# Single tiles of two edge stages fetched row by row from SP and ScalarE instead of GpSimd, with two smaller edits, in a four-layer graph network on one core

## What is computed

```python
# layer 2: one of 16 matrices by edge type, summed by destination
h_src = feat[src]
for r in range(num_rels):
    mask = etypes == r
    msg = msg + h_src * mask[:, None].astype(feat.dtype) @ weight[r]
out = jax.ops.segment_sum(msg, dst, num_segments=feat.shape[0])
# layer 3: a three-matrix network on every edge, then mean and maximum by node,
# then a three-matrix network on every node (W4, W5, W6)
m = jnp.concatenate([x[row], x[col], edge_attr], axis=1)
```

## Time and profile before

| | |
|---|---|
| median of three runs | 13071.3 us |
| the three runs | 13070.82, 13071.3, 13152.06 us |
| the profiled execution, its time | 13160.62 us |
| its span, from first to last instruction or transfer | 13158.9 us |
| PE busy | 2819.3 us (21%) |
| DVE busy | 6175.8 us (47%) |
| ACT busy | 1273.1 us (10%) |
| POOL busy | 9662.0 us (73%) |
| DMA, mean over the span | 84 GB/s |
| granted TensorE clock, mean | 0.558 of full speed |

### The profile page before, as it was taken

The page is one execution under the profiler, slowest core; times in us unless marked ns, Lnnn a source line. Parts: engine busy times, 40 slices in busy tenths (PEclk is TensorE's granted clock), DMA queues, the critical chain, the costliest instruction groups (busy, mean ns, idle before and its releaser), DMA issues. The chain is left out here.

```text
span 13158.9 us, 78994 instructions
## 1 busy us (share of the span) xinstructions
PE 2819.3 (21%) x12129; PEld 1989.0 (15%) x12156; DVE 6175.8 (47%) x21573; ACT 1273.1 (10%) x3641; POOL 9662.0 (73%) x10101
## 2 busy tenths in 40 slices
PE   2000011111100740000000000013444444444446
PEld 2000011111100420000000000012232332332233
DVE  8877357777733432222222222224555555555554
ACT  3111011111110320000000000000000000001011
POOL 7777757777777747777777777777777777777774
PEclk6555555555555665555555555555666666666665
DMA  5444334444443332222222222222222222222221
GB/s 168 119 118 115 108 106 118 117 116 118 115 119 108 124 103 66 65 66 64 67 64 67 64 67 64 67 51 55 66 66 66 66 64 66 65 66 66 66 66 32
DMA packets 731549, 1103.24 MB, mean 84 GB/s; under 512 B 240731, under 2 KB 347192, under 8 KB 730567
## 3 DMA queue, kind: packets, MB, share of 16 engines
q0 software_dynamic: 332944, 306.83, 12.6%
q1 hardware_dynamic: 231478, 567.25, 11.4%
q10 hardware_dynamic: 167040, 228.30, 5.7%
HBM read 548.64 MB, written 552.93 MB: 84 GB/s over the span
## 5 line engine op out<-in xcount | busy, mean ns | idle before, releaser
L130 POOL DMA_INDIRECT msg<-Y,idx x3125 | 2965.9, 949 | 1060.1 <-issue 951.8
L130 POOL DMA_INDIRECT g<-in_edge_attr,idxs x3072 | 2948.7, 960 | 1017.7 <-issue 858.3
L130 POOL DMA_INDIRECT yg<-ytab,idx x3125 | 2951.8, 945 | 962.4 <-issue 950.0
L1520 DVE SCALAR_TENSOR_TENSOR run<-run,same,msg 128x64 f32<-128x64 f32 x3125 | 890.7, 285 | 3030.5 <-DMA msg<-Y,idx 2923.0
L584 DVE SCALAR_TENSOR_TENSOR run<-run,sameD 128x80 f32<-128x80 f32 x3072 | 906.3, 295 | 1396.9 <-DMA g<-in_edge_attr,idxs 875.2
L1914 DVE SCALAR_TENSOR_TENSOR run<-run,same,ps 128x32 f32<-128x32 f32 x3125 | 774.9, 248 | 1640.7 <-PE ps L1808 1538.0
L1108 PE MATMUL ps<-tail,before 128*128 128x64 f32 (+2 forms) x10 | 2.8, 422 | 4575.7 <-PEq L1422 3931.0
L1897 DVE SCALAR_TENSOR_TENSOR zx<-zx,same,zs 128x32 f32<-128x32 f32 x3124 | 792.1, 254 | 136.7 <-DVE anew L1880 29.1
L588 DVE SCALAR_TENSOR_TENSOR runS<-runS,sameS,g 128x64 f32<-128x64 f32 x3072 | 850.3, 277 | 0.0
L1789 PE MATMUL ps<-eaT,W1e 128*128 128x512 f32 (+1 forms) x394 | 401.6, 1123 | 1962.7 <-DMA yg<-ytab,idx 1962.1
L952 PE MATMUL ps<-hot 128*98 128x128 bf16 x3072 | 373.1, 315 | 1891.0 <-DVE hot L680 1891.0
(11 more groups left out here) (339 smaller groups left out, 6217.2 us busy)
## 6 DMA issues: line engine op xcount, KB each, us to landing
R<-run SPq DMA_DIRECT2D x390, 320.0 KB, 2.3
R<-run SPq DMA_DIRECT2D x195, 512.0 KB, 2.7
R<-run SPq DMA_DIRECT2D x124, 800.0 KB, 3.8
v<-in_edge_attr ACTq DMA_DIRECT2D x384, 256.0 KB
RA<-runS SPq DMA_DIRECT2D x256, 256.0 KB, 3.0
Y<-tab SPq DMA_DIRECT2D x98, 512.0 KB, 2.7
msg<-Y,idx POOLq DMA_INDIRECT x3125, 2.4
Z<-zeros SPq DMA_DIRECT2D x125, 400.0 KB, 4.3
```

Of the source, the lines that this page charges most:

```text
L130: eng.indirect_dma_start(out=out, out_offset=None, in_=table, in_offset=bass.IndirectOffsetOnAxis(ap=index, axis=0)).then_inc(sem, 16)
L1520: ins_ = v.scalar_tensor_tensor(out=run[:, q, t, :], in0=prev, scalar=same[:, q, t:t + 1], in1=msg[:, q, t, :], op0=ALU.mult, op1=ALU.add)
```

## The change

1. **Row by row.** In edges_2 one tile of each slot (tile 12 of 25) is no longer gathered by POOL. Its 128 rows are fetched by 128 plain DMAs of 256 bytes each, issued by SP for the slots 0, 2 and 4 and by ACT for 1 and 3. In edges_3 one tile of a chunk of 64 (tile 8 of slot 1) is fetched so by SP, 128 bytes a row; the tail's tiles stay with POOL. The issuing engine brings 32 row addresses at a time into its registers with one load from a list in SBUF, which lies on one partition and is itself fetched from two new DRAM tensors, rows2 and rows3.
2. **The lists.** In edges_01 DVE computes the byte addresses (four short instructions more), and SP writes them to rows2 and rows3, transposed, 16640 and 6272 single numbers of 4 bytes, right behind the load of x.
3. **112 and 15.** The load of x and the three stores of the result over 127 partitions are each split in 112 and 15 partitions.
4. **nodes_3.** Four times 32 outputs are stacked on the 128 partitions, with W4 in a zero-padded band, W5 on the diagonal of a 128 x 128 matrix and W6 in four row blocks. The W5 product is one of 256 columns for 896, ACT's ReLUs are one instruction each for two, and the W6 product is three instructions for seven.
5. POOL clears three more weight tiles at the start, SP loads 16 small weight pieces more, and in edges_3 PE's wait for the gathers stands behind the first product of a slot instead of ahead of it.

```diff
+def row_bytes(ap):
+    return ap.bitcast(U8).rearrange("(o r) b -> o (r b)", o=1)
+
+def fetch_rows(nc, eng, offsets, out, table, size, sem):
+    for a in range(0, P, ROW_REGS):
+        _, rows = nc.values_load_multi_w_load_instructions(
+            offsets[0:1, a:a + ROW_REGS], engines=[eng.engine], min_val=0, max_val=table.shape[1] - size,
+            skip_runtime_bounds_check_because="the byte at which a row of the table begins")
+        for i, row in enumerate(rows):
+            eng.dma_start(out[a + i:a + i + 1, :].bitcast(U8), table[:, bass.ds(row, size)]).then_inc(sem, 16)
...
-            sp.dma_start(k.X[0:LASTP, :, :], ins["x"][0:LASTP * NB, :].rearrange("(p b) f -> p b f", b=NB)).then_inc(settled, 16)
+            for a, z in ((0, MOSTP), (MOSTP, LASTP)):
+                sp.dma_start(k.X[a:z, :, :], ins["x"][a * NB:z * NB, :].rearrange("(p b) f -> p b f", b=NB)).then_inc(settled, 16)
...
+            sp.wait_ge(rows_listed, 2)
+            for to, rows in ((k.rows2, rows2[:, :, :].rearrange("p c q -> p (c q)")), (k.rows3, rows3[:, :])):
+                sp.dma_start(to.rearrange("n p -> p n"), rows, allow_slow_non_contiguous=True).then_inc(settled, 16)
...
+        def row_tile(eng, c, q):
+            eng.wait_ge(listed[q], 16)
+            eng.sem_clear(listed[q])
+            fetch_rows(nc, eng, lists[:, q, :], msg[:, q, ROW_AT2, :], Yb, 4 * D, by_row[q])
+            list_rows(eng, c + 1, q)
...
             with sp.Fori(0, LAST) as c:
                 for q in range(NS2):
                     slot(c, q)
+                    if q in SP_ROWS:
+                        row_tile(sp, c + 1, q)
...
+                    if q not in SP_ROWS:
+                        row_tile(act, c, q)
...
                 for t in range(SL2):
+                    if t == ROW_AT2:
+                        continue
                     gather(pool, msg[:, q, t, :], k.Y, idx[:, q, t:t + 1],
...
-                            v.wait_ge(got[q], 16 * SL2 * (c + 1))
+                            v.wait_ge(got[q], 16 * (SL2 - 1) * (c + 1))
+                            v.wait_ge(by_row[q], 16 * P * (c + 1))
...
-                sp.dma_start(most[:, a:z, :], k.X[0:LASTP, a:z, :]).then_inc(saved, 16)
-                saves += 1
+                for i, j in ((0, MOSTP), (MOSTP, LASTP)):
+                    sp.dma_start(most[i:j, a:z, :], k.X[i:j, a:z, :]).then_inc(saved, 16)
+                    saves += 1
...
-                    for a, z in halves:
-                        nc.tensor.matmul(psH2[:, a:z], k.W5[:, :], h1[:, a:z], start=True, stop=True).then_inc(hid2, 1)
+                    nc.tensor.matmul(psH2, k.W5e[:, :], h1[:, :], start=True, stop=True).then_inc(hid2, 1)
```

More of the change, by code:

```diff
@@ L19 @@
 LASTN = N - LASTP * NB
+MOSTP = LASTP // 16 * 16
+STACK = P // 32
 D = 64
@@ L1434, in edges_2 @@
         stored = [sem(f"stored2_{q}") for q in range(NS2)]
+        lists = sb("lists2", [1, NS2, P], I32)
+        listed = [sem(f"listed2_{q}") for q in range(NS2)]
+        by_row = [sem(f"by_row2_{q}") for q in range(NS2)]
         late = [sem(f"msg_late{i}") for i in range(SL2 // PART2)]
@@ L1441, in edges_2, with list_rows @@
         PARTS = SL2 // PART2
+        Yb = row_bytes(k.Y)
+        def list_rows(eng, c, q):
+            eng.dma_start(lists[:, q, :], k.rows2[bass.ds(c * NS2 + q, 1), :]).then_inc(listed[q], 16)
+        def row_tile(eng, c, q):
[3 more added lines that the diff above has]
+            list_rows(eng, c + 1, q)
         def last_slot(c, q):
@@ L1454, in slot @@
                 sp.dma_start(Z[:, bass.ds(at * MSG, SL2 * MSG)], k.zeros[:, 0:SL2 * MSG]).then_inc(zero_put, 16)
+            for q in SP_ROWS:
+                list_rows(sp, 0, q)
+            for q in SP_ROWS:
+                row_tile(sp, 0, q)
             with sp.Fori(0, LAST) as c:
@@ L1479, in body @@
                     act.copy(same[:, q], k.same[:, at]).then_inc(meta_ready, 1)
+                    if q not in SP_ROWS:
+                        row_tile(act, c, q)
+            for q in range(NS2):
+                if q not in SP_ROWS:
+                    list_rows(act, 0, q)
             turns(act, CHUNKS2, body)
@@ L1710, in edges_3, with by_rows @@
         anew = sb("anew", [P, NS3, SL3])
+        lists = sb("lists3", [1, P], I32)
+        listed, by_row = sem("listed3"), sem("by_row3")
+        ytab = row_bytes(k.ytab)
+        def by_rows(c, q):
+            return q == ROW_SLOT3 and not (isinstance(c, int) and c == CHUNKS3)
         loaded = [sem(f"loaded3{q}") for q in range(NS3)]
@@ L1743, in store, with list_rows, row_tile @@
                 sp.dma_start(R3[:, bass.ds(c * CH3 + q * SL3, steps), :], run[:, q, 0:steps]).then_inc(stored[q], 16)
-            with sp.Fori(0, CHUNKS3) as c:
+            def list_rows(c):
+                sp.dma_start(lists[:, :], k.rows3[bass.ds(c, 1), :]).then_inc(listed, 16)
+            def row_tile(c):
+                sp.wait_ge(listed, 16)
+                sp.sem_clear(listed)
+                fetch_rows(nc, sp, lists[:, :], yg[:, ROW_SLOT3, ROW_AT3 * MSG:(ROW_AT3 + 1) * MSG], ytab, 4 * MSG, by_row)
+                list_rows(c + 1)
+            list_rows(0)
+            row_tile(0)
+            with sp.Fori(0, LAST) as c:
                 for q in range(NS3):
                     store(c, q)
+                    if q == ROW_SLOT3:
+                        row_tile(c + 1)
+            for q in range(NS3):
+                store(LAST, q)
+            sp.wait_ge(listed, 16)
             for q, steps in enumerate(TAILS3):
@@ L1760, in slot @@
                 for t in range(steps):
+                    if by_rows(c, q) and t == ROW_AT3:
+                        continue
                     gather(pool, yg[:, q, t * MSG:(t + 1) * MSG], k.ytab, idx[:, q, t:t + 1], got[q])
@@ L2010, in _ @@
         def _(pe):
-            nc.tensor.matmul(k.ps[0:MSG, 7, 0:1], k.W4u[:, :], k.u3[:, :], start=True, stop=True).then_inc(ubs, 1)
+            nc.tensor.matmul(k.ps[:, 7, 0:1], k.W4u[:, :, :].rearrange("p j f -> p (j f)"), k.u3[:, :], start=True,
+                             stop=True).then_inc(ubs, 1)
             def turn_rows(g, q):
@@ L2028, in output @@
                 hold(pe, hid2_r, g + 1, k.passed)
-                for b in range(GB):
-                    last = nc.tensor.matmul(psY[q][:, b * D:(b + 1) * D], h2[:, b * P:(b + 1) * P], k.W6[:, :],
-                                            start=False, stop=b == GB - 1)
-                last.then_inc(outp, 1)
+                both = psY[q][:, 0:(GB - 1) * D].rearrange("p (j c f) -> p j c f", c=2, f=D)
+                nc.tensor.matmul(both[:, :, 1, :], h2[:, P:2 * P], k.W6e[:, 0:STACK - 1, :], start=False, stop=False)
+                nc.tensor.matmul(both[:, :, 0, :], h2[:, 0:P], k.W6e[:, 0:STACK - 1, :], start=False, stop=False)
+                nc.tensor.matmul(psY[q][:, (GB - 1) * D:], h2[:, 0:P], k.W6e[:, STACK - 1, :], start=False, stop=True)\
+                    .then_inc(outp, 1)
             def body(c, ahead):
@@ L2036, in body @@
                     g = 2 * c + q
-                    for i, (a, z) in enumerate(halves):
+                    for i, stacks in enumerate(((0, 1), (3, 2))):
                         pe.wait_ge(turned_c, 2 * g + i + 1)
-                        nc.tensor.matmul(psH[:, a:z], k.W4a[:, :], catT[:, a:z], start=True, stop=True).then_inc(hid, 1)
+                        for j in stacks:
+                            n = min(2, GB - 2 * j) * P
+                            last = nc.tensor.matmul(psH[:, 0:n], k.W4z[:, (STACK - 1 - j) * MSG:(2 * STACK - 1 - j) * MSG],
+                                                    catT[:, 2 * j * P:2 * j * P + n], start=j == 0, stop=j == 2)
+                    last.then_inc(hid, 1)
                     if later(c, q):
```

67 lines of the change are left out of this document (44 added, 23 removed).

## The result

The changed kernel takes 13268.6 us (median of 4 runs, 13241.75 to 13369.98), the kernel before 13071.3: a ratio of 1.015, 95% interval 1.0094 to 1.0205. It is slower, by 197 us. The forecast was 12730, faster, so the prediction is wrong in sign.

What follows compares the result with a forecast made beforehand. POOL's issuing of gathers was taken to bound both edge stages. Terms of -147, -60, -65, -28, -47 and +2 us sum to -345, which from the median of 13071 gives 12726, rounded 12730; range 12650 to 13000.

Steps and rivals of the forecast that it cites:

- What bounds the kernel: Both edge stages: POOL's issuing sets the pace, a gather taken from it is worth 1.25 us unless another engine becomes slower.
- stage 2: edges_2: 125 gathers less at 1.2537 us are 156.7 us; after a 10 us allowance, -147 us.
- the load of 32 addresses: SP's row tiles in edges_2: one register load taken as 1.0 us, between 0.05 and 2.4, 4.0 us a tile.
- what SP has to do in 150.4 us: edges_2: SP's three row tiles and ten stores a chunk take 147.5 us, 3 us under POOL's 150.4.
- break-even of 48.4: edges_2: a row tile on SP must stay under 48.4 us for SP to keep under POOL; 47.4 was predicted.
- the slower one: Rival, edges_2: a row tile takes SP over 53 us, needing a load of 2.4 us or rows at 0.38; chance 0.16.
- The pace of a row: SP's row DMAs in edges_2: 0.335 us each, 42.9 us for the 128 of a tile.
- Stage 3: edges_3: 48 gathers less at 1.2492 us, -60 us.
- The load of x: Load of x and lists: spread over 16 engines, lists 50 us, 14 us lost for 78.9, so -65 us.
- nodes_3 and the end: nodes_3: 14 passes of 9.5 us for 11.5, -28 us; end: last store some 4 us for 50.9, -47 us.
- gathers slowed by small packets: Rival: row fetches slow POOL's gathers by 0.03 us each, 180 us in all, time 12910; chance 0.05.
- lists as dear as W2r: Rival, at the load of x: writing the lists costs what W2r did, +112 us, time 12840; chance 0.08.

Runs made afterwards that it cites:

- f3: Changed kernel with no row tile in either edge stage and no lists, the rest of the change kept: 12910.0 us, ratio 0.988 to the kernel before.
- f2: Changed kernel with SP fetching slots 0 and 2, ACT 1 and 3, slot 4's tile back on POOL: 12746.7 us, ratio 0.9754 to the kernel before.
- g3: Changed kernel with each chunk's fifth row tile shared, rows 0 to 63 by SP, 64 to 127 by ACT: ratio 0.9743 to the kernel before.
- g2: Changed kernel with constant row addresses and no address loads (fetches wrong rows): 12714.7 us, ratio 0.972 to the kernel before.
- f4: Changed kernel with 16 addresses to a register load instead of 32: 13388.8 us, ratio 1.0247 to the kernel before.
- g4: f3's kernel, but with the two lists of addresses still written: 12933.5 us, ratio 0.9888 to the kernel before.
- f1: The changed kernel unaltered, run again on another chip: 13266.5 us, ratio 1.0149 to the kernel before.
- g1: Changed kernel with SP keeping its three row tiles a chunk and ACT's two back on POOL: 13253.9 us, ratio 1.0129 to the kernel before.

## Why the prediction was wrong

**What bounds the kernel** was read rightly: POOL's issuing, 1.25 us a gather, with everybody else waiting. Against f3, f2 gives back 127 us of stage 2 for 100 gathers and g3 158 us for 125, 1.27 us each, and from f2 to g3 it is 31.3 us for 25, 1.25 us.

**The step that failed is the load of 32 addresses**, in the part on what SP has to do in 150.4 us. It had been bounded by 0.05 and 2.4 us, and 1.0 was taken. It measured 2.13 at the median, and behind stores 4.2, above the upper bound. Adding up SP's instructions from start to start over 19 turns of its loop in the trace of after gives, us a chunk:

| | predicted | after |
|---|---|---|
| 384 rows | 128.7 | 128.2 |
| 12 loads of 32 addresses | 12.0 | 32.4 |
| fetches of the lists | 1.5 | 1.4 |
| ten stores with their address work | 5.3 | 8.4 |
| end of the loop's body | none | 2.8 |
| sum | 147.5 | 173.2 |

Of the 25.7 us too few, 20.4 are the loads: nine of them take 19.6 us and the three behind stores 12.8. The stores, taken at the price of the earlier trace rows, cost 3.1 us more where two slots' stores stand back to back. The loop's end was in no term; the earlier trace rows hid it, since SP waited anyway. Over the stage, 25 x (172.1 - 156.7) = 385 of the 390 us lost. With loads of 1.0 us and all else as measured, the turn would be 152.8 us, over POOL's 150.4 but under the 156.7 of before: stage 2 would have gained about 25 x 3.9 = 98 us (an estimate). So the loads decide the sign, as g2 shows by experiment, and the two other items would have taken a third of the gain.

The choice behind the step was worse than the number. A tile of 47.4 us against a break-even of 48.4 left 1 us, and the load stood four times in it: at 1.25 us a load the gain begins to go, and the range of its bounds reached to 2.4. The text named the load as its weakest number and gave the loss a chance of 0.16. By its own bounds, even weight between 0.05 and 2.4 puts half of the cases over that break-even. The rival that happened is the slower one, a row tile over 53 us on SP, and by the condition that it gave: it wanted a load of 2.4 us, and the mean of the twelve is 2.70 (32.4 / 12). Measured as the prediction counts, a tile is 55.6 us ((172.1 - 5.3) / 3), at which its sum, 13071 - 198 + 25 x 15.4 = 13258, is 11 us from the result.

The Trainium skill, Runtime: NRT & Kernel Launch, section Instruction fetch mechanics, gives about 200 ns for a register of a TENSOR_LOAD from HBM. The runs here, where the list lies in SBUF, disagree in size, with 56 ns a register and 0.337 us for the load, but its statement that the price goes by the register even in bulk is what f4 shows.

**The pace of a row** came out right, 0.335 us taken and 128.2 / 384 = 0.334 measured, but by luck: the prediction took the DMA alone and no instruction beside it. The trace has a MOVE, 0.062 us from its start to the DMA's, and a DMA that is shorter than its likeness of the earlier trace rows, 0.272 us to what follows. The two errors cancel.

**Stage 3**: -60 predicted. The gathers of yg span 3849.2 us in after against 3902.6, -53; f2 against f3 gives -59.

**The load of x**: -65 predicted, with 50 us for the lists and 14 lost. The stretch of the lists on the queues was 64 us (1597.8 to 1661.9) and 22.4 were lost, so -57. The spreading of x itself did what it should: in f3 the wait is gone.

**nodes_3 and the end**: -28 and -47 predicted. The last 3.4 us for 50.9 are -47.5. From the first gather of nodes_3 to the end of the span are 156.5 us for 238.6, -82 in all, so the passes and what stands around them gave -35, the outer end of their range. (The first gather is that of fix_rows, at 12920.3 before and at 13211.6 after.) PE, by line and form, in after (busy us, mean ns; compare):

```profile
L2148 PE MATMUL ps<-nh,W5e 128*128 128x256 f32 x28 | 13.7, 587 | 0.0
L2127 PE MATMUL ps<-W6e,nh 128*128 128x192 f32 x28 | 8.3, 378 | 0.0
L2128 PE MATMUL ps<-W6e,nh 128*128 128x192 f32 x28 | 6.8, 326 | 0.0
L2129 PE MATMUL ps<-W6e,nh 128*128 128x64 f32 x28 | 4.6, 247 | 0.0
```

W5 fell from 46.1 to 13.7 us, W6 from 34.7 to 19.7. I had reckoned with a lower clock level in these passes; the granted clock rose from 0.56 to 0.71.

All terms but stage 2 summed to -198; f3 with g4's lists and stage 3's tile gives 13067 - 157 + 23 - 59, or -193. That the sum is so near owes something to luck: the parts missed by 7, 8 and -7 us in the profiles. So one term of six was wrong, and it outweighed the rest. The other rivals (gathers slowed by small packets, lists as dear as W2r) are refuted: 944 to 947 ns a gather in every run at this pace, and 23 us.

## What to carry to other kernels

Work moved to an idle engine's instruction list pays only while that list, with everything in it, stays shorter than the bound: put a price to every instruction of it (loads of registers, stores back to back, what stands behind a store, the loop's end), and where the margin is smaller than the spread of one unknown price, take the smaller dose. Here four tiles gave 0.975 and five gave 1.015, and five with half a tile moved over gave the full gain of stage 2 (158 us for 156.7 forecast). The sign to look for in a profile is which engine has ceased to wait: SP's 3750 us of waiting were its reserve, and when that row is gone, SP is the bound.

## What the runs showed that was not expected

- Loading registers from a list in SBUF takes 0.337 us and 56 ns for each register on SP (1.232 us for 16 in f4, 2.127 for 32), and 2.24 us for 32 on ScalarE.
- Behind a slot's stores (R<-run of 800 KB, and the zeros) such a load takes 4.2 us at the median (3.6 to 5.2), and of 16 addresses 3.3. In g2 a DMA with a constant address follows within 0.11 us, but can itself be long (1.64 us for 0.25). The cause is open.
- The MOVE that a register address needs costs 0.062 us from start to start, but a row DMA behind it takes 228 ns at the median against 254 with a constant address, so a fixed address saves little: 0.334 us a row against 0.318 to 0.325 in two undisturbed tiles.
- On one chip the same kernels lost time in pauses of the engines' instruction lists: the kernel before took 15796 us instead of 13067, and the four tiles that win on the other chips (0.975) lose there (1.180). The median of a row DMA is the same, its maximum is not. Of the kernels run there, those with more instructions lost more.
- The late start of stage 2 goes with TensorE's granted clock in the stage of dense matmuls ahead of it. The windows from 4300 to 4600 us of after (late start) and, in the second fence, of f1:

```profile
4300.00:4600.00 300.00, 262.58 (x894) 137.60 (x911) 145.79 (x273) 127.16 (x185) 208.34 (x210) 0.70 0.45 147
```

```profile
4300.00:4600.00 300.00, 249.88 (x1133) 132.31 (x1132) 180.23 (x341) 159.80 (x231) 222.53 (x224) 0.92 0.53 176
```

At a granted clock of 0.70 894 matmuls are done in 300 us, at 0.92 1133; both are mixtures of the engine's two levels, 1.2 and 2.4 GHz. In the window from 4400 to 4500 us the four profiles with the late start (before, after, g1, g3) have 0.69 to 0.70 and the six others 0.85 to 0.97. What sets the mixture was not tried. The prediction had considered POOL's wait at the load of x as a cause of this excess; that was wrong, since up to 4200 us g1 and g3 run as g2 does (VectorE does 4529 instructions between 1600 and 4200 us in each).
